# A separate ring of eight edge-list slots ahead of the four slots of gathered rows in a fused graph-attention kernel

## The chip, the cores and the metric

The program runs on one core of one Trainium2 chip. The core has five engines with a queue of instructions each: TensorE (PE, with its weight loads PEld), VectorE (DVE), ScalarE (ACT), GpSimd (POOL) and SyncE (SP), and 16 DMA engines that all of them share. The metric is the time of one execution on the device in microseconds, the median of several runs.

## What is computed

6250 nodes with 256 features and 200000 edges (src, dst), sorted by dst. The destinations are dense for low node numbers and thin out towards high ones. The layer norm of x feeds two branches: three graph-attention layers one behind the other, and a linear-attention block. Their sum is added to x, and a second layer norm feeds a feed-forward block of 8 experts with the two best weighted. The part that this case is about, the graph layer:

```python
def _gat_layer(x, W, al, ar, b, src, dst, apply_act):
    h = (x @ W).reshape(N_NODES, HEADS, HEAD_DIM)
    el = jnp.einsum('nhd,hd->nh', h, al)
    er = jnp.einsum('nhd,hd->nh', h, ar)
    e = jax.nn.leaky_relu(el[src] + er[dst], negative_slope=NEG_SLOPE_ATTN)
    m = jax.ops.segment_max(e, dst, num_segments=N_NODES)
    ex = jnp.exp(e - m[dst])
    s = jax.ops.segment_sum(ex, dst, num_segments=N_NODES)
    a = ex / s[dst]
    msg = h[src] * a[:, :, None]
    out = jax.ops.segment_sum(msg, dst, num_segments=N_NODES)
```

## The kernel before, in words

Nodes are cut into 49 tiles of 128 (loop variable `T`), edges into slots of 512 (`g`), each slot four chunks of 128 edges (`c`). For each of the three layers (`l`) a table in DRAM has, for each node, a row of 280 floats: the projected features with a one behind each head, and the logit terms. A *pair* (`n`) is one slot seen from one tile. As edges are sorted, a tile takes a few neighbouring slots: 57 pairs in tile 0, 24 in tile 1, 5 or 6 in the last ones, 440 pairs for 393 slots in a layer. The last slot of a tile is, at 47 of the 48 borders, also the first slot of the next (a *shared* slot); it is loaded and gathered once and used by two pairs. The control table `ctl` has a row per tile: the edge at which it starts, the first slot that it does not share (`unshared`), its last slot, `shift` (pair number minus slot number), its first slot, and two cuts of its slots into thirds, behind which other work is put.

The work of a slot goes through the engines like this:

- SP (L320 to L335) waits until the slot's ring place is free, loads `meta` (src and dst of 512 edges, 4 KB) and `dstb` (the 512 destinations as 16-bit numbers, copied to all 128 partitions, 128 KB), waits until both have landed and raises `meta_ready`. There are four places for everything (`RING`). The place is free when the messages of the pair four pair numbers back are done: `msg_ready` at L327 counts with the shift of the tile whose slot is loaded. At a shared border the first three new slots of a tile thereby wait for a pair later than the one that last used their place.
- POOL (L375 to L384) waits for `meta_ready` of the next slot, issues four indirect DMAs that gather 128 rows of the table each into `gat`, and behind the third of them announces the slot *before* (`gathered`, L360), once its rows have landed. So the announcement of slot g stands behind the wait for the edge list of slot g+1.
- DVE (`logits`, `messages`) waits for `uv_ready` of PE and for `gathered`, adds logits (`lg`, L955, L958), compares destinations for the next pair (`selT`, L943, from `dstb`), builds four selection matrices (`sel`, L963, from `meta`, each half behind `agg_done` of the pair before), waits for ACT's exponentials and multiplies the rows (`msg`, L972, two halves, each raising `msg_ready`).
- ACT (`weigh`) makes the exponentials (L471, L473).
- PE (`pairs`): `prepare(n + 1)` (L1225, 12 small matmuls out of `selT`), then `aggregate(n)` (L1249): two halves, each behind its `msg_ready`, of sel x msg, summed in `acc`. `after(part)` puts other work between thirds of a tile: the next layer's projection and the linear attention in layers 0 and 1, the experts (L1177, L1188) in layer 2.

Each engine takes its instructions in order; loops have run-time bounds.

## Time and profile before

| | |
|---|---|
| Median of three runs | 9743.75 us (9727.61 to 9778.39) |
| The profiled execution, its own time | 9719.24 us |
| Its span, first to last instruction | 9717.4 us |
| Mean granted TensorE clock | 0.803 |
| Busy: PE / DVE / POOL / ACT | 65% / 52% / 46% / 20% |
| Layer 0 / 1 / 2, about | 200 to 3160 / 3160 to 6130 / 6130 to 9650 us |

In the page, L12 is line 12 of the kernel. "Idle before" is how long an engine stood idle ahead of an instruction, and "<-" names what ended that: another engine's instruction and line, a DMA, "issue" where the profile shows no wait, and "remote" where a semaphore rose at that moment and the profile has no instruction that ended just then to put it down to. In the chain of waits the same appears as "another core or an unknown queue". The suffix q (SPq, POOLq, PEldq) marks the queue's own instructions. A row of the timeline merges repeats of one instruction.

### The profile page before, as it was taken

The numbers are of one execution on the slowest core, as the hardware profiler recorded it, in microseconds if no ns is written. First come the engines' busy times: TensorE is split into PE (matmuls) and PEld (weight loads), VectorE is DVE, ScalarE is ACT, GpSimd is POOL, SyncE is SP. The second block draws the span as 40 slices with busy tenths as digits, with TensorE's granted clock in tenths as the row PEclk, the third lists the DMA queues.
The fourth block names the chain that finished last, engine by engine and source line by source line (L and its number), as shares of the span: only waits on it lengthen the run. The fifth ranks groups of instructions, "written<-read, shape, count | busy, mean of one in ns | idle before, by whom it ended". The sixth has DMA issues, their size and how long they took to land.

```text
span 9717.4 us, 172782 instructions
## 1 busy us (share of the span) xinstructions
PE 6287.2 (65%) x38910; PEld 4899.6 (50%) x38911; DVE 5020.9 (52%) x14572; ACT 1955.3 (20%) x5913; POOL 4475.7 (46%) x4723
## 2 busy tenths in 40 slices
PE   3555555666666455555556566455777888889899
PEld 2434444444444333434444444334566667777778
DVE  4444555555555454555555566444554555555554
ACT  1000000101111000000000000001333444555555
POOL 0555554544444555555444444455444443333332
PEclk8677777777787676777777777777888899999999
DMA  4443433433333344333333333443333232222221
GB/s 157 109 106 99 103 101 101 106 96 98 99 100 93 102 106 99 101 101 98 98 97 97 98 98 96 94 104 99 92 89 83 78 78 76 74 72 70 66 67 44
DMA packets 638578, 909.85 MB, mean 94 GB/s; under 512 B 271425, under 2 KB 484554, under 8 KB 638410
## 3 DMA queue, kind: packets, MB, share of 16 engines
q0 software_dynamic: 226368, 676.39, 26.8%
q1 hardware_dynamic: 369546, 192.99, 8.4%
q10 hardware_dynamic: 42624, 40.02, 1.2%
q8 instruction: 16, 0.26, 0.0%
q14 instruction: 24, 0.20, 0.0%
HBM read 868.05 MB, written 40.87 MB: 94 GB/s over the span
## 4 chain that ended last, share of the span: by engine, by line
PE 28%; issue 18%; another core or an unknown queue 16%; DVE 15%; DVEq 12%; DMA 4%; ACT 4%; SPq 2%; ACTq 1%; POOL 1%; POOLq 0%
PE bank L1249 17%; DVE msg L972 6%; PE bank L1177 5%; PE bank L1188 4%; DVE sel L963 4%; DMA dstb<-dst_d 3%; DVEq L237 3%; DVEq L963 1%; DVE lg L955 1%; ACT region L429 1%; ACT L466 1%; DVEq L943 1%; DVEq L955 1%; SPq L328 1%
## 5 line engine op out<-in xcount | busy, mean ns | idle before, releaser
L353 POOL DMA_INDIRECT gat<-table,meta x4716 | 4474.7, 949 | 5152.8 <-SPq L335 3529.1
L1249 PE MATMUL bank<-msg,sel 128*128 128x264 f32 x10560 | 3667.1, 506 | 1751.7 <-DVE msg L972 1335.7
L1249 PEld LDWEIGHTS bank<-msg,sel 128*128 128x128 f32 x10560 | 2482.9, 247 | 2375.9 <-DVE msg L972 1432.7
L963 DVE TENSOR_SCALAR sel<-kc,base_i,meta 128x128 f32<-128x128 f32 x5280 | 1565.3, 355 | 1470.0 <-remote 799.9
L972 DVE TENSOR_TENSOR msg<-gat,bank 128x528 f32<-128x528 f32 x2640 | 1732.2, 697 | 576.5 <-ACT bank L473 480.2
L471 ACT ACTIVATE ex<-lg 128x32 f32<-128x32 f32 x1320 | 298.8, 226 | 6040.5 <-DVE lg L958 4609.5
L1225 PE MATMUL bank<-uvb,selT 128*128 (+1 forms) x15876 | 672.1, 172 | 1166.5 <-DVE selT L943 681.4
L1225 PEld LDWEIGHTS bank<-uvb,selT 128*128 128x128 bf16 x15876 | 617.0, 100 | 1566.9 <-issue 932.0
L955 DVE TENSOR_TENSOR lg<-gat,bank 128x64 f32<-128x64 f32 x1320 | 288.9, 219 | 1712.0 <-remote 901.4
L1177 PE MATMUL bank<-xT,w 128*128 128x128 f32 x6272 | 790.9, 281 | 18.0 <-issue 18.0
L1188 PE MATMUL bank<-w,region 128*128 128x256 f32 x3136 | 773.6, 390 | 42.2 <-ACT region L429 24.4
L1177 PEld LDWEIGHTS bank<-xT,w 128*128 128x128 f32 x6272 | 771.0, 197 | 49.0 <-issue 32.9
L1188 PEld LDWEIGHTS bank<-w,region 128*128 128x128 f32 x3136 | 577.1, 194 | 139.4 <-issue 41.1
L429 ACT ACTIVATE region<-bank,b 128x128 f32<-128x128 f32 x1568 | 443.8, 370 | 995.2 <-PE bank L1177 682.9
L943 DVE TENSOR_SCALAR selT<-dstb,kc 128x512 bf16 (+1 forms) x1323 | 498.3, 377 | 266.6 <-issue 158.3
L958 DVE TENSOR_TENSOR lg<-lg 128x32 f32<-128x32 f32 x1320 | 256.3, 194 | 112.3 <-issue 15.6
L1157 PE MATMUL bank<-zb 128*128 128x264 bf16 (+1 forms) x298 | 102.0, 344 | 323.3 <-DVE xn L986 243.2
L429 ACT ACT_TABLE_LOAD x237 | 304.1, 1283 | 6.0
L466 ACT ACT_TABLE_LOAD x236 | 302.8, 1283 | 4.3
L473 ACT ACTIVATE bank<-ex 128x32 f32<-128x32 f32 x1320 | 265.4, 201 | 89.9
L806 DVE SCALAR_TENSOR_TENSOR region<-bank,region 128x256 f32 (+1 forms) x343 | 165.2, 482 | 141.6 <-PE bank L1188 63.7
L1157 PEld LDWEIGHTS bank<-zb 128*128 128x128 bf16 x298 | 32.2, 108 | 345.5 <-DVE xn L986 252.4
(184 smaller groups left out, 2435.7 us busy)
## 6 DMA issues: line engine op xcount, KB each, us to landing
dstb<-dst_d SPq DMA_DIRECT2D x1179, 128.0 KB
gat<-table,meta POOLq DMA_INDIRECT x4716
meta<-in_edges SPq DMA_DIRECT2D x1179, 4.0 KB
table<-hrow ACTq DMA_DIRECT2D x98, 140.0 KB
w<-in_W SPq DMA_DIRECT2D x2, 4096.0 KB
table<-hrow SPq DMA_DIRECT2D x49, 140.0 KB, 1.8
region<-xnT_d ACTq DMA_DIRECT2D x50, 128.0 KB
region<-qT_d ACTq DMA_DIRECT2D x50, 128.0 KB
```

What stands on the lines that cost most here:

```text
L353: pool.indirect_dma_start(gat[:, r, c, :], None, table[l], bass.IndirectOffsetOnAxis(meta[:, r, c, 0:1].bitcast(U32), 0)).then_inc(s_done, 16)
L429: last = act.activation(gT[:, e % 2, k, :], bank[5 + e % 2][:, k * P:(k + 1) * P], ACT.Gelu, bias=b1[:, e * HB + k:e * HB + k + 1])
L466: act.activation(warm[:, 1:2], warm[:, 0:1], ACT.Exp)
L471: act.activation(ex[:], lg[:], ACT.Relu, scale=-1.0)
L943: dve_v.tensor_scalar(selT[:], dstb[:, bass.ds(g % RING, 1), :].rearrange("p a e -> p (a e)"), node[:, bass.ds(T, 1)], None, ALU.is_equal) ...
L955: dve_v.tensor_tensor(lg2[:], rows_of(g)[:, :, MSG:ROW], uv_p[:, 0:CH * UV].rearrange("p (c w) -> p c w", w=UV), ALU.add)
L963: dve_v.tensor_scalar(sel[:, c, :], iota, base_i[:, bass.ds(T, 1)], meta[:, bass.ds(g % RING, 1), c, 1:2].rearrange("p a w -> p (a w)"), A ...
L972: dve_v.tensor_tensor(msg[:, cs, :].rearrange("p c (h d) -> p c h d", h=H), rows_of(g)[:, cs, 0:MSG].rearrange("p c (h d) -> p c h d", h=H ...
L1177: last = pe.matmul(bank[5 + e % 2][:, k * P:(k + 1) * P], w1[:, e, c, k * P:(k + 1) * P], xT[:, 0, c, :], start=(c == 0), stop=(c == 1))
L1188: last = pe.matmul(y_psum[e % 2][:, 0:C], gT[:, e % 2, k, :], w2[:, e, k, :], start=(k == 0), stop=(k == HB - 1))
L1225: last = pe.matmul(uv_p[:, c * UV:(c + 1) * UV], selT[:, c * P:(c + 1) * P], uvb[:, part, bass.ds(T, 1), :].rearrange("p a b -> p (a b)"), ...
L1249: last = pe.matmul(acc[:, 0:MSG], sel[:, c, :], msg[:, c, :], start=False, stop=False)
```

## The change

The edge lists and broadcast destinations (`meta`, `dstb`) get a ring of `AHEAD` = 8 places, apart from the four of `gat`. SP's loop becomes: wait until the load before has landed; load `meta` and `dstb` of slot g; then wait until slot g-5 and all before it have been used up (`slot_free`, a new semaphore that starts at 8); then raise `meta_ready`. POOL gathers slot x when `meta_ready` is x+2 (before: x+1), which stands for three things: the edge list of x has landed, that of x+1 has been issued, and slot x-4 is used up. Who says that a slot is used up changes as well: before it was DVE's `msg_ready`; now PE raises `slot_free` by one in `aggregate`, behind its wait for the second half of the messages and ahead of the second half's matmuls. A tile's last pair raises nothing; the first pair of the next tile does it, once for a shared slot and twice otherwise, in a small loop with run-time bounds (`release_first`). POOL's loop is unrolled over eight slots instead of four, and the padding of slots goes to a multiple of 8 and one instead of 4 and one. That is the same 393 slots for these edges: 392 real ones and one of padding. `small` is cut from 512 to 256 columns to make room.

```diff
@@ SyncE, per layer @@
+                sp.sem_inc(meta_in[l], 16)
+                sp.sem_inc(dst_in[l], 16)
                 with sp.Fori(0, NT) as T:
                     with sp.Fori(unshared, last + 1) as g:
                         edge = edges_of(g, start, first)
-                        r = g % RING
-
-                        sp.wait_ge(msg_ready[l], 2 * (g + shift) + 2)
+                        r = g % AHEAD
+
+                        landed = sp.snap(16 * (g + 1))
+                        sp.wait_ge(meta_in[l], landed)
+                        sp.wait_ge(dst_in[l], landed)
                         sp.sem_inc(slot_taken, 1)
                         sp.dma_start(meta[...]).then_inc(meta_in[l], 16)
                         sp.dma_start(dstb[...]).then_inc(dst_in[l], 16)
-                        sp.wait_ge(meta_in[l], 16 * (g + 1))
-                        sp.wait_ge(dst_in[l], 16 * (g + 1))
+
+                        sp.wait_ge(slot_free[l], g + (AHEAD - RING))
                         sp.sem_inc(meta_ready[l], 1)
@@ GpSimd @@
-                pool.wait_ge(meta_ready[l], 1)
+                pool.wait_ge(meta_ready[l], 2)
                 for c in range(CH):
-                    gather_row(0, c, slot_in[l][0])
+                    gather_row(0, 0, c, slot_in[l][0])
                 with pool.Fori(0, rounds) as i:
-                    for j in range(RING):
-                        r = (j + 1) % RING
-                        pool.wait_ge(meta_ready[l], RING * i + j + 2)
+                    for j in range(AHEAD):
+                        m, r = (j + 1) % AHEAD, (j + 1) % RING
+                        pool.wait_ge(meta_ready[l], AHEAD * i + j + 3)
                         pool.sem_inc(round_taken, 1)
                         for c in range(CH):
-                            gather_row(r, c, slot_in[l][r])
+                            gather_row(m, r, c, slot_in[l][r])
                             if c + 2 == CH:
-                                announce(j, i + 1)
+                                announce(j % RING, 2 * i + j // RING + 1)
@@ VectorE @@
-                dve.sem_inc(msg_ready[l], AHEAD)
+                dve.sem_inc(slot_free[l], AHEAD)
                 def selectT(g, T):
-                    dve.wait_ge(meta_ready[l], g + 1)
+                    dve.wait_ge(meta_ready[l], g + 2)
@@ TensorE @@
-                def aggregate(n):
+                def aggregate(n, release):
                     for h in range(2):
-                        pe.wait_ge(msg_ready[l], 2 * n + (AHEAD + h + 1))
+                        pe.wait_ge(msg_ready[l], 2 * n + (h + 1))
+                        if h == 1:
+                            release()
                         for c in range(h * HALF, (h + 1) * HALF):
                             last = pe.matmul(acc[:, 0:MSG], sel[:, c, :], msg[:, c, :], start=False, stop=False)
+                    def release():
+                        pe.sem_inc(slot_free[l], 1)
+
+                    def release_first():
+                        if opening:
+                            release()
+                        else:
+                            pe.sem_inc(tile_opened, 1)
+                            with pe.Fori(unshared, first + 2):
+                                release()
+
                     prepare(n0 + 1, T)
-                    aggregate(n0)
+                    aggregate(n0, release_first)
                     for part, (begin, end) in enumerate(((n0 + 1, n1), (n1, n2), (n2, n3))):
                         with pe.Fori(begin, end) as n:
                             prepare(n + 1, T)
-                            aggregate(n)
+                            aggregate(n, release)
                     prepare(n3 + 1, T + 1)
-                    aggregate(n3)
+                    aggregate(n3, lambda: None)
```

## Rows read from the trace of the kernel before

**Rows 1.** The page's head: span, and busy time and share by engine.

```profile
span 9717.4 us, 172782 instructions
PE 6287.2 (65%) x38910; PEld 4899.6 (50%) x38911; DVE 5020.9 (52%) x14572; ACT 1955.3 (20%) x5913; POOL 4475.7 (46%) x4723
```

**Rows 2.** Stretches of the layers: length, busy PE, PEld, DVE, ACT, POOL, clock.

```profile
200.00:3160.00 2960.00, 1735.56 (x9994) 1268.59 (x9994) 1530.44 (x4472) 275.12 (x1174) 1491.69 (x1572) 0.75 0.40 101
3160.00:6130.00 2970.00, 1654.98 (x9796) 1233.75 (x9796) 1609.21 (x4428) 234.83 (x1077) 1490.88 (x1572) 0.73 0.39 98
6130.00:9650.00 3520.00, 2752.93 (x18391) 2294.21 (x18392) 1780.68 (x5379) 1374.12 (x3385) 1492.09 (x1572) 0.89 0.32 81
```

**Rows 3.** The page's chain that ended last, by engine.

```profile
PE 28%; issue 18%; another core or an unknown queue 16%; DVE 15%; DVEq 12%; DMA 4%; ACT 4%; SPq 2%; ACTq 1%; POOL 1%; POOLq 0%
```

**Rows 4.** Groups by line: busy, mean ns, idle before, by releaser.

```profile
L353 POOL DMA_INDIRECT gat<-table,meta x4716 | 4474.7, 949 | 5152.8 <-SPq L335 3529.1 <-issue 1591.5 <-DMA gat<-table,meta 15.6
...
L963 DVE TENSOR_SCALAR sel<-kc,base_i,meta 128x128 f32<-128x128 f32 x5280 | 1565.3, 355 | 1470.0 <-remote 799.9 <-PE bank L1249 481.3 <-issue 181.6
...
L955 DVE TENSOR_TENSOR lg<-gat,bank 128x64 f32<-128x64 f32 x1320 | 288.9, 219 | 1712.0 <-remote 901.4 <-issue 517.6 <-POOLq L360 166.2
```

**Rows 5.** Who waited on POOL's announcements (line 360), whole span: us, times.

```profile
  DVE lg L955: 211.1, 116
```

**Rows 6.** Timeline, layer 0, tile 2's end (last logits at 871.03).

```profile
861.95 1.30 DVE L972 TENSOR_TENSOR msg<-gat,bank 128x528 f32<-128x528 f32 x2
...
865.81 0.35 SPq L328 DMA_DIRECT2D meta<-in_edges  x1
...
867.69 2.05 PE L1249 MATMUL bank<-msg,sel 128*128 128x264 f32 x8 [1.12 <-DVE msg L972]
...
870.03 0.94 POOL L353 DMA_INDIRECT gat<-table,meta  x1 [5.39 <-SPq L335]
...
871.03 0.22 DVE L955 TENSOR_TENSOR lg<-gat,bank 128x64 f32<-128x64 f32 x1 [2.05 <-POOLq L360]
```

**Rows 7.** Timeline, start of layer 1.

```profile
3163.27 0.57 DVE L923 CAST uvb<-gat 128x784 bf16<-128x784 f32 x1
3164.38 0.34 SPq L328 DMA_DIRECT2D meta<-in_edges  x1
3164.93 0.34 SPq L330 DMA_DIRECT2D dstb<-dst_d  x1
3168.05 0.35 DVE L943 TENSOR_SCALAR selT<-dstb,kc 128x512 bf16<-128x512 uint16 x1 [4.21 <-SPq L335]
3168.29 0.94 POOL L353 DMA_INDIRECT gat<-table,meta  x1 [34.76 <-SPq L335]
```

**Rows 8.** PE's queue: loop branches, event instructions (ns min/median/max).

```profile
L1262 PEldq COMPARE_BRANCH  x1026: 67/207/222, 223.1 to 9640.5; - x171
...
L1183 PEldq EVENT_SEMAPHORE  x343: 51/51/51, 6701.7 to 9707.5; - x172
```

**Rows 9.** Timeline: a slow stretch in tile 0, layer 0.

```profile
526.97 0.60 DVE L963 TENSOR_SCALAR sel<-kc,base_i,meta 128x128 f32<-128x128 f32 x2 [3.90 <-remote]
...
531.88 0.60 DVE L963 TENSOR_SCALAR sel<-kc,base_i,meta 128x128 f32<-128x128 f32 x2 [4.32 <-remote]
```

**Rows 10.** Three stretches around it, columns as in group 2.

```profile
521.00:527.00 6.00, 0.46 (x12) 0.37 (x12) 0.82 (x4) 0.43 (x2) 4.57 (x5) 0.84 0.54 135
527.00:533.00 6.00, 0.00 (x0) 0.00 (x0) 1.68 (x5) 0.00 (x0) 2.99 (x4) 0.50 0.38 105
533.00:538.00 5.00, 4.20 (x20) 3.09 (x20) 2.79 (x10) 0.43 (x2) 0.00 (x0) 0.50 0.14 27
```

**Rows 11.** The page's DMA queues: gathers (q0), SP's transfers (q1).

```profile
q0 software_dynamic: 226368, 676.39, 26.8%
q1 hardware_dynamic: 369546, 192.99, 8.4%
```

**Rows 12.** SP's own waits, whole span: us in total, times, longest.

```profile
SPq L335 <- DMA dstb<-dst_d: 2433.0, 1109, 3.4
```

## What the change should do: the prediction, made blind

> **What bounds the kernel now.** I read the page's head first [rows 1]: no engine is full. PE is busy for 65% of the span, DVE for 52%, POOL for 46%. The stretches of the layers [rows 2] say where: in layers 0 and 1, PE and DVE are each busy for 52% to 59% of the time, POOL for half; in layer 2, with the experts, PE is at 2752.93 of 3520 us (78%). So the time of layers 0 and 1 is that of a chain which passes through several engines, and that of layer 2 is closer to PE's own. The chain of waits [rows 3] agrees: PE 28%, DVE 15% and its queue 12%, "another core or an unknown queue" 16%, and DMA 4%, SPq 2%, POOL 1%. What the change speeds up (SP, its loads, POOL) has a small part of it.
>
> POOL's row [rows 4] tempts to another reading: it idles for 5152.8 us, 3529.1 of them until SP raised `meta_ready` (L335). That idleness costs nothing unless someone waits for what POOL announces. So the next view is who waited on the announcements [rows 5]: DVE's logits (L955), 211.1 us, 116 times. The row of the logits themselves, seen from DVE's side [rows 4], gives them 166.2 us of idle time. That is 1.7% of the span and the pool from which the change can draw. Most of DVE's idleness is another: 901.4 us ahead of the logits and 799.9 us ahead of `sel` are "remote".
>
> Where the 166.2 us lie, the timeline at the end of tile 2 shows [rows 6]. The last pair's logits start at 871.03, after 2.05 us of waiting for L360. The announcement stands behind POOL's wait for the *next* slot's edge list, and those gathers started at 870.03, after 5.39 us in which POOL waited for SP. SP had issued the load at 865.81, for a ring place given free by the messages that ended at 861.95 + 1.30 = 863.25; by the late rule for shared borders that is one pair more than needed. I went through all pairs of the three layers: announcements that came over 0.5 us behind the messages before them are 76, nearly all at the last pair of a tile, and the others are in the first slots of a layer. Their waits sum to 118 us, and with the shorter ones to 137 us.
>
> **The slow stretches.** The "remote" waits matter as the ground against which everything here runs. Two halves of `sel` start at 526.97 and 531.88, each 3.90 or 4.32 us late [rows 9]. The wait between them is for four chunks' worth of half a pair on PE, for 4.9 us. In 521 to 533 POOL gathers without a pause (busy 4.57 of 6 us, then 2.99 of 6) and PE and DVE get almost nothing done; in 533 to 538 POOL rests and PE does 4.20 us of work in 5 [rows 10]. The DMA engines aren't full: their share is 0.54 and 0.38 in the slow stretches [rows 10]. Over all time slices, I find DVE in such a wait in about one slice in seven while POOL has gathered for less than 5 us on end, and in about half of them when it has for longer. This is a coincidence in time, not a shown cause.
>
> **The change part by part.** All sums are against the profiled execution, 9719.24 us (span 9717.4); it lies 24.5 us (0.25%) under the median of 9743.75, and the predicted time is the median plus the same difference.
>
> *The load leaves the path from a free place to its gathers, and the extra pair at shared borders goes.* Before: from SP's issue at 865.81 to the gathers 4.22 us [rows 6], and at the start of a layer 3168.29 - 3164.38 = 3.9 us [rows 7]. After: the list is there already, and the same event lets POOL start at once. Together with the pair saved (about 6.7 us: 2960 us for 440 pairs [rows 2]) the announcement at a tile's end comes some 10 us earlier, against a wait of 1.65 us in the mean (166.2 in 101 waits). These waits go as a whole. What is late next is PE: in [rows 6] its sums for the pair before began at 867.69 and need 2.05 us at the full clock, so it is done at 869.7, and `sel` of a pair whose logits start 2 us earlier meets that end without a wait; at half the clock the same work takes 3.9 us, which eats most of the gain. Mean clock is 0.73 to 0.89 [rows 2]. I take two thirds of 166.2 as recovered: -111 us (bounds: -50, and -211 if all of [rows 5] goes).
>
> *Start of a layer.* The first load goes out before DVE has finished the reference logits, and `meta_ready` = 2 asks only for the issue of the second. Before, `selT` started at 3168.05 and the gathers at 3168.29, after logits that ended at 3163.27 + 0.57 = 3163.84 [rows 7]. After, two issues (0.34 us each, 0.2 between them) and POOL's start of about 0.8 us (before, 3164.93 + 0.34 and 2.2 us of landing [rows 12] make 3167.5, and POOL starts at 3168.29): 2.5 us less, three times, -8 us. The gathers of the next slots are bound by one load after the other as before.
>
> *SP.* It has one load in flight at a time, as before; landing costs it 2433.0 us of waiting in 1109 waits, 2.2 us each [rows 12], now while nobody needs it. Its cycle of about 5 us for a slot is under the 7.5 us for which a slot lasts (2960 us for 393). Costed at nothing; the cover is that difference.
>
> *PE's release.* An instruction of 51 ns [rows 8] on PE's queue for each of 1320 pairs. It waits for the second half of the messages, and only the second half's matmuls are queued behind it; before, the first of those held the same wait. Cover: the four chunks of the first half, 1.0 us, against messages that come 0.65 us after the first half's (1.31 for both). At each tile's first pair the small loop comes on top, with a branch of 207 ns at the median [rows 8] and some register instructions of 40 ns, in all 0.34 us, 147 times: 50 us uncovered at the full clock, nothing at half of it. I take +15 us. In a slow stretch every instruction of PE's is dear: half a pair's four chunks, eight instructions and their loads, took the 4.9 us of [rows 9], 0.6 us each. My 1320 + 8 x 147 = 2500 instructions are 3.2% of PE's 77821 [rows 1]; 3.2% of the 901.4 + 799.9 = 1701 us [rows 4] is 55 us. Bounds 0 and 55, taken +30 us, since DVE's waits aren't all for PE. The release also follows PE's order now: if PE is late, the place comes free late, by up to the 4.9 us of [rows 9]. Who waits for that is SP, then POOL, then an announcement that has come 10 us earlier, of which its waits need 2 to 4; costed at nothing.
>
> *POOL and DVE.* POOL's loop over eight slots saves half of its loop ends, and DVE's instructions stay the same. Nothing, both.
>
> Sum: -111 - 8 + 15 + 30 = **-74 us**: 9645 us for the profiled execution, **9670 us** for the median.
>
> *A rule against it.* After the change, each slot's load travels beside gathers, where before POOL stood waiting for it. The loads hold 8.4% of the DMA engines' time and the gathers 26.8% [rows 11]; 8.4% of 9717 us over 1179 slots is 0.7 us of all engines for a slot, which the 6 us or more that the announcement now has to spare swallow. The Trainium skill, "DMA: Bandwidth & Descriptors", section "Queues, rings and completion order", says that a DMA engine takes turns, packet by packet, between the queues that have work, so a load in the same moment does slow a gather. By that rule, too, the sum stays as it is; only where the turns reach the engines' own work, as rival 2 has it, would it change.
>
> **The rivals.** *Rival 1: the wait changes its name.* The 111 us are taken by what comes next at the tile's end (PE at half clock, a slow stretch that the gathers now fall into), and the additions to PE remain. For it: "remote" and "issue" waits at L955 are 1419.0 us, eight times those for POOL [rows 4]; DVE is nearly always held by something else. Price: -50 + 45 - 8 = -13 us, 9731 us. Against: at the tile's end in [rows 6], PE is no later than DVE.
>
> *Rival 2: the gathers run on end, and slow stretches grow.* Before, SP's cycle of load and landing puts a pause between bunched gathers (5.39 us in [rows 6]); the change takes these pauses away, and POOL follows each release at once. If gathers without a pause are the cause of the slow stretches [rows 9, 10], their 1701 us grow. It decides from a growth of 4% (74 us); with 12%, +204 us, the sum is +130 us: 9874 us; with 9%, 9823. Laying the new rule over the old times of release, I find POOL's time in runs over 10 us on end up by a fifth in layers 0 and 2 and down a little in layer 1, worth between 0 and +100 us by the shares above. Against: the gathers' sum, the places for rows and the pairs' pace stay, and POOL's total of 4474.7 us [rows 4] is the same; runs on end happen when PE and DVE are fast, and end when the four places are full.
>
> *Rival 3: it does more than it says.* Gathers spread evenly and ahead take a part of the slow stretches with them: 8% of 1701 is -136 us, with the sum -210 us: 9534 us.
>
> *That it doesn't do what it says* could be only if POOL's idle time until SP stayed. The order of waits excludes that in a steady run: the load of the next slot is issued two slots' use ahead, 15 us, of which it needs 5.
>
> **How the numbers follow.** Forecast (9600 to 9695, a gain of 50 to 145 us): 0.43. Rival 1 (9695 to 9790): 0.31. Rival 2 (over 9790): 0.20. Rival 3 (under 9600): 0.06. The range that leaves out two in ten: from 9575, which takes in half of rival 3, up to 9825, where two thirds of rival 2 lie below (its 0 to +100 us and PE's upper bounds). A measurement of this kernel can tell 0.5% (49 us) from no change. Faster by more: 0.43 + 0.06 = 0.49. Within: 0.31. Slower by more: 0.20.
>
> **What would show it right or wrong.** In the profile after: waits of DVE's logits for POOL under 40 us instead of 166; POOL's idle time no longer put down to SP after a landing, but to SP after a release from PE; SP's waits for landings gone or small, waits for `slot_free` in their place; logits at a tile's last pair with no wait over 1 us; selT and the first gathers of a layer 2 to 3 us behind L923. Right for rival 1: the same, with the span as before and "remote", "issue" and PE's rows larger by 100 us. Right for rival 2: "remote" ahead of L955 and L963 clearly over 1701 us in sum, and gathers in longer rows. Wrong altogether: waits for POOL as large as before, or PE idle ahead of L1249's second halves by some tenths of a microsecond each, the price of the release where I hid it.

## The result, and the profile after

The changed kernel takes **10094.1 us** at the median of 4 runs (10083.29 to 10096.91), the kernel before 9745.04 us on the same chip: ratio **1.0352**, 95% interval 1.0323 to 1.0381. It is slower by 3.5%; 9670 us was forecast and 9825 us was the upper end of the range. Run twice more, the change gave 1.0363 (1.0321 to 1.0405) and, on a chip where the kernel before takes only 7759.59 us, 0.9961 (0.9947 to 0.9976). This second kind of chip has a section of its own below; where nothing is said, a run comes from a chip on which the kernel before takes 9727 to 9875 us.

The head of the page of the changed kernel, and its chain of what ended last, answering [rows 1] and [rows 3]:

```profile
span 10081.5 us, 174415 instructions
PE 6430.9 (64%) x38910; PEld 5010.5 (50%) x38911; DVE 5049.9 (50%) x14572; ACT 1960.1 (19%) x5913; POOL 4495.8 (45%) x4723
...
PE 31%; another core or an unknown queue 22%; issue 15%; DVE 14%; DVEq 11%; ACT 5%; ACTq 1%; DMA 0%; SPq 0%; POOL 0%; POOLq 0%; PEldq 0%
```

DMA and SPq have left the chain (4% and 2% before), as they were meant to. "Another core or an unknown queue" has grown from 16% to 22%. The stretches of the layers, with the columns of [rows 2]:

```profile
200.00:3240.00 3040.00, 1738.64 (x9994) 1275.49 (x9994) 1534.62 (x4471) 276.08 (x1174) 1499.49 (x1572) 0.76 0.39 98
3240.00:6256.00 3016.00, 1710.62 (x9796) 1267.40 (x9796) 1610.11 (x4429) 234.90 (x1077) 1499.33 (x1572) 0.73 0.39 97
6256.00:10014.00 3758.00, 2837.92 (x18390) 2364.78 (x18391) 1804.69 (x5380) 1377.76 (x3384) 1495.91 (x1572) 0.87 0.31 76
```

Every layer is longer: by 80, 46 and 238 us. The granted clock differs by 0.02 at most (0.89 before and 0.87 now in layer 2, where PE is busy for 85 us more), so it explains a small part at best. The groups by line, answering [rows 4]: gathers, PE's sums, `sel`, logits:

```profile
L371 POOL DMA_INDIRECT gat<-table,meta x4716 | 4494.7, 953 | 5492.7 <-SPq L347 4081.8 <-issue 1367.9 <-remote 31.0
L1269 PE MATMUL bank<-msg,sel 128*128 128x264 f32 x10560 | 3793.7, 518 | 2420.9 <-DVE msg L990 1849.6 <-issue 565.1
L981 DVE TENSOR_SCALAR sel<-kc,base_i,meta 128x128 f32<-128x128 f32 x5280 | 1566.1, 352 | 2223.0 <-remote 1395.6 <-PE bank L1269 635.2 <-issue 176.3
L973 DVE TENSOR_TENSOR lg<-gat,bank 128x64 f32<-128x64 f32 x1320 | 287.2, 218 | 1519.5 <-remote 915.3 <-issue 493.9 <-PE bank L1243 78.1
```

The busy times of POOL's and DVE's rows stand still (within 20 us each). PE's sums are busy for 126.6 us more, in records whose ends are modelled; their row before was this:

```profile
L1249 PE MATMUL bank<-msg,sel 128*128 128x264 f32 x10560 | 3667.1, 506 | 1751.7 <-DVE msg L972 1335.7 <-issue 415.9
```

What moved most are the idle times. "Remote" ahead of `sel` rose from 799.9 to 1395.6 us, ahead of the logits from 901.4 to 915.3: 1701.3 to 2310.9, **+610 us, or 36%**. Against it, the logits have 192.5 us less of idle time in all (1712.0 to 1519.5). Their waits for POOL are gone, in the table of waits:

```profile
DVE lg L973 <- POOLq L378: 24.5, 33, 7.3
```

It was 166.2 us in 101 waits [rows 4]. So the part that the change aims at works: 142 us of these waits are gone, where the sum had 111. SP's own waits (us in total, times, longest) show the rest of the design, against 2433.0 us of waits for landings [rows 12]:

```profile
SPq L347 <- PEq L1278: 1938.5, 475, 10.1
SPq L347 <- PEq L1285: 1536.8, 144, 20.1
SPq L339 <- DMA dstb<-dst_d: 301.8, 246, 2.6
```

And the start of layer 1, answering [rows 7]:

```profile
3243.63 0.57 DVE L941 CAST uvb<-gat 128x784 bf16<-128x784 f32 x1
3245.19 0.34 SPq L340 DMA_DIRECT2D meta<-in_edges  x1
3245.74 0.36 SPq L342 DMA_DIRECT2D dstb<-dst_d  x1
3246.26 0.35 DVE L961 TENSOR_SCALAR selT<-dstb,kc 128x512 bf16<-128x512 uint16 x1 [2.06 <-SPq L347]
3246.49 0.95 POOL L371 DMA_INDIRECT gat<-table,meta  x1 [39.13 <-SPq L347]
```

From the end of L941 to the first gather it is 2.29 us (3246.49 - 3244.20); before it was 3168.29 - 3163.84 = 4.45. That is 2.2 us saved, and at the starts of layers 0 and 2 it is 2.0 us each; 2.5 us were forecast.

A stretch of layer 0 shows what the added waits are. Timeline of the changed kernel, with the wait ahead of each row in brackets:

```profile
2029.84 2.05 PE L1269 MATMUL bank<-msg,sel 128*128 128x264 f32 x8 [1.13 <-issue]
...
2031.34 0.95 POOL L371 DMA_INDIRECT gat<-table,meta  x1 [0.53 <-issue]
...
2032.02 0.60 DVE L981 TENSOR_SCALAR sel<-kc,base_i,meta 128x128 f32<-128x128 f32 x2
2032.20 0.66 PE L1243 MATMUL bank<-uvb,selT 128*128 x12 [0.31 <-DVE selT L961]
2032.59 0.95 POOL L371 DMA_INDIRECT gat<-table,meta  x1 [0.30 <-issue]
2033.84 0.95 POOL L371 DMA_INDIRECT gat<-table,meta  x1 [0.30 <-issue]
2034.54 0.70 SPq L340 DMA_DIRECT2D meta<-in_edges  x1
2035.10 0.95 POOL L371 DMA_INDIRECT gat<-table,meta  x1 [0.30 <-issue]
2037.38 0.01 SPq L342 DMA_DIRECT2D dstb<-dst_d  x1
2037.56 0.60 DVE L981 TENSOR_SCALAR sel<-kc,base_i,meta 128x128 f32<-128x128 f32 x2 [4.94 <-remote]
```

The second half of `sel` needs the second half of the sums that PE began at 2029.84. By PE's record they end at 2031.89, and PE begins the next pair's matmuls at 2032.20; DVE sees the semaphore at about 2037.5. The same wait stands in [rows 9]. SP is slow here too: its two issues are 2.84 us apart, at the layer's start 0.55. POOL is not: its gathers start every 1.25 us as always. The Trainium skill, "Perfetto Trace Analysis", section "Tensor Engine Instruction (MATMUL, LD_WEIGHTS)", says that the end of a matmul is computed by the profiler, and that the semaphore is raised only when PSUM has acknowledged the bytes. This row agrees in so far as end and semaphore are over 5 us apart; whether the work or its announcement is late, it can't tell. The record of the semaphores in the same trace puts the delay on PE's side: the last matmul of the sums raises its semaphore at 2037.41, and the last of the twelve matmuls begun at 2032.20 (by its record over at 2032.86) raises another at 2037.59, while DVE's own, raised by `selT` (over at 2032.06), comes at 2032.08. DVE isn't slow here; it waits. Around it, stretches with the columns of [rows 2]:

```profile
2026.00:2032.00 6.00, 4.76 (x26) 3.35 (x24) 3.80 (x12) 0.34 (x3) 4.45 (x5) 0.73 0.47 113
2032.00:2038.00 6.00, 0.66 (x12) 0.51 (x12) 1.06 (x5) 0.09 (x1) 3.13 (x4) 0.83 0.54 137
2038.00:2043.00 5.00, 4.17 (x10) 3.15 (x11) 2.12 (x6) 0.42 (x2) 0.00 (x0) 0.52 0.04 10
```

It is the picture of [rows 10]: a slow stretch of 5 us while POOL gathers, and work as soon as it rests. But POOL gathers in the first of the three too, at full pace for PE and DVE. Counted over the trace, the waits of over 3.5 us ahead of a half of `sel` went from 84 to 193, in 2640 halves (223 in c1, a second run of the same kernel).

### The profile page after: what moved, and what is told of

Read it like the earlier page. It is cut to its first block, busy times and chain, and to the rows that moved or that the text cites. A ratio compares the mean times of both kernels' runs of the same rounds, so it can differ in the third digit from the quotient of the medians.

```text
span 10081.5 us, 174415 instructions
## 1 busy us (share of the span) xinstructions
PE 6430.9 (64%) x38910; PEld 5010.5 (50%) x38911; DVE 5049.9 (50%) x14572; ACT 1960.1 (19%) x5913; POOL 4495.8 (45%) x4723
## 4 chain that ended last, share of the span: by engine, by line
PE 31%; another core or an unknown queue 22%; issue 15%; DVE 14%; DVEq 11%; ACT 5%; ACTq 1%; DMA 0%; SPq 0%; POOL 0%; POOLq 0%; PEldq 0%
PE bank L1269 21%; DVE msg L990 6%; PE bank L1195 5%; DVE sel L981 4%; PE bank L1206 3%; DVEq L239 3%; DVEq L981 1%; ACT L484 1%; ACT region L447 1%; DVE lg L973 1%; ACT L447 1%; DVEq L1009 1%; PE bank L1243 1%; DVE region L1049 1%
## 5 line engine op out<-in xcount | busy, mean ns | idle before, releaser
L1269 PE MATMUL bank<-msg,sel 128*128 128x264 f32 x10560 | 3793.7, 518 | 2420.9 <-DVE msg L990 1849.6
L1269 PEld LDWEIGHTS bank<-msg,sel 128*128 128x128 f32 x10560 | 2542.2, 253 | 3098.1 <-DVE msg L990 1950.0
L981 DVE TENSOR_SCALAR sel<-kc,base_i,meta 128x128 f32<-128x128 f32 x5280 | 1566.1, 352 | 2223.0 <-remote 1395.6
L1243 PE MATMUL bank<-uvb,selT 128*128 (+1 forms) x15876 | 646.5, 172 | 793.3 <-DVE selT L961 486.8
L973 DVE TENSOR_TENSOR lg<-gat,bank 128x64 f32<-128x64 f32 x1320 | 287.2, 218 | 1519.5 <-remote 915.3
L1195 PE MATMUL bank<-xT,w 128*128 128x128 f32 x6272 | 846.1, 290 | 99.0 <-issue 98.6
L1195 PEld LDWEIGHTS bank<-xT,w 128*128 128x128 f32 x6272 | 813.1, 204 | 147.5 <-issue 131.6
L1149 PE MATMUL bank<-wext,xT 128*128 128x280 f32 x588 | 178.7, 429 | 3.0 <-ACT xT L496 0.9
```

The lines of the kernel that those rows point to most:

```text
L973: dve_v.tensor_tensor(lg2[:], rows_of(g)[:, :, MSG:ROW], uv_p[:, 0:CH * UV].rearrange("p (c w) -> p c w", w=UV), ALU.add)
L981: dve_v.tensor_scalar(sel[:, c, :], iota, base_i[:, bass.ds(T, 1)], meta[:, bass.ds(g % AHEAD, 1), c, 1:2].rearrange("p a w -> p (a w)"), ...
L1195: last = pe.matmul(bank[5 + e % 2][:, k * P:(k + 1) * P], w1[:, e, c, k * P:(k + 1) * P], xT[:, 0, c, :], start=(c == 0), stop=(c == 1))
L1243: last = pe.matmul(uv_p[:, c * UV:(c + 1) * UV], selT[:, c * P:(c + 1) * P], uvb[:, part, bass.ds(T, 1), :].rearrange("p a b -> p (a b)"), ...
L1269: last = pe.matmul(acc[:, 0:MSG], sel[:, c, :], msg[:, c, :], start=False, stop=False)
```

## The experiments

The theory after the result (T) is that the loss is made by the gathers, and by *where in a pair's work* they start: the new rule starts them early, and they then fall on PE's sums and on the first half of the next pair. Its rivals: the instructions added to PE's queue (P); the release that now follows PE's order (O); and slow stretches that have nothing to do with gathers (N).

### Is it the gathers at all?

**g1_one_gather.** The kernel before, with one gather of four. It leaves out three quarters of the gathered rows, so its output isn't the layer's; a constant stands in their place.

```diff
-                        for c in range(CH):
-                            gather_row(r, c, slot_in[l][r])
-                            if c + 2 == CH:
-                                announce(j, i + 1)
+                        gather_row(r, 0, slot_in[l][r])
+                        announce(j, i + 1)
```

> The kernel before with one gather of 128 rows for each slot instead of four; chunks 1 to 3 of the rows keep a constant that is written once a layer, so three quarters of the gathered data are left out. Everything else runs as before. If the gathers make the slow stretches (waits put down to 'remote' ahead of logits and sel, 1701 us in the kernel before): under 400 us of them, and the time 7800 to 8700 us. If they come from elsewhere (SyncE's loads, PE itself): over 1200 us of them, and 9400 to 9700 us.

A single execution took 7654.02 us, beside 9727.17; that is less than the lowest of the range that was expected. Its sums, `sel` and logits by line:

```profile
L1248 PE MATMUL bank<-msg,sel 128*128 128x264 f32 x10560 | 3271.2, 462 | 1054.4 <-DVE msg L971 1049.4 <-issue 5.0
L962 DVE TENSOR_SCALAR sel<-kc,base_i,meta 128x128 f32<-128x128 f32 x5280 | 1519.9, 343 | 333.7 <-PE bank L1248 329.6
L954 DVE TENSOR_TENSOR lg<-gat,bank 128x64 f32<-128x64 f32 x1320 | 289.1, 219 | 1214.8 <-POOLq L360 784.2 <-issue 257.1 <-PE bank L1224 165.7
```

"Remote" is gone from both of DVE's lines. All else of the pair's work, and SP's 193 MB of loads, is there. N falls: on this chip, three quarters of the gathers cost the kernel about 2070 us, while the logits' waits for POOL were 166.2 us before [rows 4] (and are 784.2 us in g1, where the announcement stands behind the only gather). Whether it is POOL's issuing or the 507 MB that the gathers move, this run doesn't tell.

### PE's release taken apart

In the cuts below, the number added behind the slot differs from run to run because each semaphore starts from its own value. Lines left out are marked with three dots.

**a1_dve_release.** The change, but the place is given free by the messages, as in the kernel before; nothing added on PE.

```diff
-                        sp.wait_ge(slot_free[l], g + (AHEAD - RING))
+                        sp.wait_ge(msg_ready[l], 2 * (g + shift) + 2)
```

> The changed kernel, with the release taken off PE: SyncE waits for msg_ready (raised by VectorE's messages) of the same pair, as the kernel before did, and PE's instructions are those of the kernel before. The eight-slot ring, the early loads and the early gathers stay. Theory 1 (early gathers: they now start with PE's sums of the same pair and lengthen the slow stretches there): as slow as the changed kernel or slower, since gathers start up to 1 us earlier still: 10050 to 10200 us. Theory 2 (the release instruction on PE, which holds up PE's queue, is the loss): the loss goes and the gain of the earlier announcements is left: 9620 to 9720 us.

**a2_before_pe_release.** The kernel before, plus the change's instructions on PE (each pair's `sem_inc`, the loop at a tile's first pair), which nobody waits for.

```diff
+                        if h == 1:
+                            release()
```

> The kernel before with PE's release instructions alone: PE raises slot_free behind the wait for the second half of the messages, and in the small loop at a tile's first pair, but nobody waits for it. Ring, loads and gathers are those of the kernel before. Theory 1: 9745 to 9800 us (at most the 15 + 30 us of the prediction). Theory 2: 10000 to 10150 us.

**a3_late_release.** The change, with PE's release behind the second half's matmuls in program order.

```diff
-                        if h == 1:
-                            release()
                         for c in range(h * HALF, (h + 1) * HALF):
...
                         last.then_inc(agg_done[l], 1)
+                    release()
```

> The changed kernel with PE's release moved behind the matmuls of the second half, so that it holds no matmul of the pair up. The gathers start some 1 us later in program order. Theory 1: as slow as the changed kernel, 10000 to 10150 us. Theory 2: most of the loss goes, 9650 to 9800 us.

**a7_dve_release_pe_extra.** a1 with a2's instructions on PE.

> The kernel with the release by VectorE's messages (9900 us) with PE's release instructions put back, raising a semaphore for which nobody waits. If the 190 us between that kernel and the changed one are the price of PE's instructions: 10050 to 10130 us. If they come from where the gathers start (the release by PE comes later, or later still in a slow stretch) and the instructions cost the 0.4% that they cost in the kernel before: 9900 to 9960 us.

| kernel | us | ratio to before (95%) | remote ahead of `sel` / logits, us |
|---|---|---|---|
| a1, messages release | 9899.77 | 1.0156 (1.0112 to 1.0200) | 1375.3 / 642.1 |
| a2, before with PE's extras | 9790.87 | 1.0040 (1.0014 to 1.0066) | 784.9 / 966.3 |
| a3, release in program order behind the sums | 10089.85 | 1.0342 (1.0294 to 1.0389) | 1409.6 / 868.5 |
| a7, a1 with PE's extras | 9937.15 | 1.0234 (1.0186 to 1.0282) | 1323.9 / 703.1 |

P has a size: 0.4% in a2, and 0.8% by a7 against a1 (the two intervals overlap, and the runs are from two chips). It isn't the cause. With nothing on PE, a1 is still slower than before by 1.6%, and its remote waits sum to 2017 us. That is between its two expectations: neither all of the loss stays nor all of it goes. a3 equals the change in time, and its gathers lie where the change's do (the table in the next section): in these runs a bare `sem_inc` behind the matmuls in program order releases no later than one ahead of them, so it doesn't tell that the sums are done. What separates a7 (1.0234) from the change (1.0352) is only which event frees the place: one pair earlier at shared borders, and PE's queue for DVE's messages. That is 1.2%, and O may hold it; the run meant to split it (a13) comes below.

### Gathers tied to the sums

**a4_sums_release.** The change, but SP waits for the semaphore on the last matmul of the pair's sums (`agg_done`). Nothing added on PE.

```diff
-                        sp.wait_ge(slot_free[l], g + (AHEAD - RING))
+                        sp.wait_ge(agg_done[l], 2 * (g + shift) + 4)
```

> The changed kernel, but SyncE lets POOL gather only when PE's sums of the pair that used the slot have ended (it waits for agg_done, raised by the last matmul), with no release instruction on PE. Gathers so start 1 to 4 us after the messages, behind the sums of their pair, and 1 to 4 us earlier than in the kernel before. Theory 1, if it is the meeting of gathers with the sums of the same pair that costs: most of the loss goes, 9650 to 9850 us; if it is run-on gathers wherever they lie: 9950 to 10150 us. Theory 2: 9620 to 9720 us. This run is of use beside the first one, which has no release on PE either.

**a6_half_sums.** As a1, and then the first half's sums as well.

```diff
-                        sp.wait_ge(slot_free[l], g + (AHEAD - RING))
+                        used = sp.snap(2 * (g + shift) + 2)
+                        sp.wait_ge(msg_ready[l], used)
...
+                        sp.wait_ge(agg_done[l], used + 1)
```

> As the kernel whose gathers wait for the end of the sums (9270 us), but SyncE waits for msg_ready of the pair and for the first half of its sums alone, so that the gathers meet the second half of the sums. No release instruction on PE. Theory 1a (the loss is in the overlap of gathers with the sums of the same pair, in proportion): between the two neighbours, 9270 and 9900 us, at about 9500 to 9700 us. Theory 1b (what counts is only that the gathers are tied to PE's progress at all, so that a slow stretch stops the gathers that make it): near 9270 us, under 9400 us.

**b1_before_sums_release.** The kernel *before* (four places, load behind the release), with a4's wait.

```diff
-                        sp.wait_ge(msg_ready[l], 2 * (g + shift) + 2)
+                        sp.wait_ge(agg_done[l], 2 * (g + shift) + 6)
```

> The kernel before, ring of four and load behind the release, with the one difference that SyncE waits for the end of PE's sums of the pair (agg_done) and not for its messages. The gathers start 1 to 4 us later than before. If the gain of 4.9% is that of a release tied to the sums, whatever the ring: 9300 to 9550 us. If it needs the early load of the eight-slot ring (gathers right behind the sums, before the next pair's): 9700 to 9950 us, since the announcements at the tile ends come later still.

| | freed by messages | freed by the end of the sums |
|---|---|---|
| load behind the release (4 places) | 1 (kernel before, 9745) | b1: 10004.85 us, 1.0321 (1.0262 to 1.0380) |
| list loaded ahead (8 places) | a1: 9899.77 us, 1.0156 (1.0112 to 1.0200) | **a4: 9270.07 us, 0.9505** (0.9464 to 0.9547) |

a6 lies beside a4: 9314.49 us, 0.9594 (0.9549 to 0.9640), in the range expected if the tie to PE's progress is what counts. Each of the two edits alone makes the kernel slower, and both together make it 5% faster than before. Neither a4 (under all of its ranges) nor b1 (over both) was forecast. Rows of a4, then of b1, by line:

```profile
L981 DVE TENSOR_SCALAR sel<-kc,base_i,meta 128x128 f32<-128x128 f32 x5280 | 1551.2, 356 | 1044.4 <-PE bank L1267 467.0 <-remote 349.6 <-issue 218.2
L973 DVE TENSOR_TENSOR lg<-gat,bank 128x64 f32<-128x64 f32 x1320 | 287.7, 218 | 1833.8 <-remote 1196.8 <-issue 362.4 <-POOLq L379 165.0
```

```profile
L963 DVE TENSOR_SCALAR sel<-kc,base_i,meta 128x128 f32<-128x128 f32 x5280 | 1563.0, 355 | 1400.8 <-remote 672.0 <-PE bank L1249 543.9 <-issue 181.1
L955 DVE TENSOR_TENSOR lg<-gat,bank 128x64 f32<-128x64 f32 x1320 | 289.6, 219 | 2143.8 <-remote 1027.9 <-issue 504.1 <-POOLq L360 493.6
```

In a4, the remote waits ahead of `sel` are a quarter of the change's; of the long ones (over 3.5 us) 7 are left of 193. But those ahead of the logits are the largest of all, 1196.8 us. The two together are 1546.4 us, only 155 us under the kernel before (1701.3), while the span is 444 us shorter (9272.9); the rest of the gain lies in no single row. In b1 the load stands between the sums and the gathers, and the logits wait for POOL for 493.6 us, 327 us more than before; its remote waits sum to 1699.9 us, as before. So b1's loss goes with the waits for POOL, and not, as the change's, with remote waits. Worked out from the starts of all gathers, the share of time in which POOL gathers, by the time from the start of a pair's messages:

| from messages' start, us | -1..0 | 0..1 | 1..2 | 2..3 | 3..4 | 4..5 | 5..6 | 6..7 |
|---|---|---|---|---|---|---|---|---|
| before | .57 | .57 | .68 | .66 | .64 | .59 | .51 | .65 |
| change | .50 | .49 | .46 | .69 | .83 | .80 | .84 | .86 |
| c1, the change again | .50 | .49 | .46 | .69 | .83 | .80 | .85 | .87 |
| a3 | .50 | .50 | .47 | .67 | .83 | .81 | .84 | .87 |
| a1 | .48 | .43 | .35 | .78 | .86 | .85 | .87 | .89 |
| a4 | .53 | .76 | .73 | .71 | .68 | .63 | .63 | .73 |
| a6 | .72 | .71 | .68 | .65 | .63 | .66 | .73 | .78 |
| b1 | .58 | .64 | .64 | .60 | .60 | .68 | .74 | .71 |

Change, a3 and a1 pack the gathers from 2 us behind the messages' start on; before, a4 and a6 spread them. How long the gathers run on end is a poorer guide. Counting gathers whose starts lie under 2 us apart as one run, the share of their time in runs of over 10 us is 53% before, 65% in a1, 75% in the change, 43% in a4, 50% in a6 and 62% in b1; but c1, the change again at the same time and with the same remote waits (2280.9 us), has 62%.

T fits these runs in this form: released with the messages and with the list at hand, the gathers come in a pack that falls on the sums and the next `sel`. Shown is that the event which releases them makes a difference of 6% (a1 against a4); that the overlap is the way in which it does is argued from the table. Whether the place in time counts, or that a4's gathers can't run ahead of PE, these runs don't separate.

### Spacing the gathers out

Three kernels put a pause between gathers, to see whether the pack is what hurts: **a5_paced** (the change), **a9_sums_paced** (a4), and **a8_fixed_delay** (a1, the pause only ahead of a slot's four, six times).

```diff
                             gather_row(m, r, c, slot_in[l][r])
+                            pool.drain()
+                            pool.memset(pace[:], 0.0)
```

> The changed kernel with a drain and a small memset (some 0.3 us) on POOL behind each gather, so that four gathers take some 6.5 us and not 5.0. If it is the rate of gathers back to back that makes the slow stretches: under 9850 us (changed kernel: 10094). If only the overlap with the sums counts and not the rate: 10050 to 10200 us.

> The kernel whose gathers wait for the end of the sums (9270 us), with the pause of 0.3 us behind each gather. A candidate for a faster version: if the rate counts beside the tie, 9000 to 9200 us; if it doesn't, 9270 to 9400 us, as the announcements then come later.

> The kernel with the release by VectorE's messages (9900 us), with six drains and memsets on POOL ahead of each slot's gathers: a fixed delay of 2 to 4 us between release and gathers. If the gain of the release by sums is one of phase alone (gathers 2 to 4 us later): 9250 to 9500 us. If it needs the tie to PE's progress (in a slow stretch no new gathers start until PE is through): 9750 to 10050 us.

18942.48 us (1.9203, 1.9124 to 1.9282), 18504.27 us (1.8762, 1.8685 to 1.8839) and 11967.45 us (1.2131, 1.2081 to 1.2180): they failed as experiments, since the pause was far longer than the memset in it. POOL's rows in a8:

```profile
1000.02 0.94 POOL L373 DMA_INDIRECT gat<-table,meta  x1 [0.30 <-issue]
1003.12 2.37 POOL L402 MEMSET pace<- 128x240 f32 x6 [2.16 <-issue]
```

Between the gather and the memset, where the drain stands, POOL is idle for 2.16 us. With a drain behind each gather POOL became the bound, as a5's rows show:

```profile
L984 DVE TENSOR_SCALAR sel<-kc,base_i,meta 128x128 f32<-128x128 f32 x5280 | 1478.4, 362 | 11.7 <-PE bank L1272 1.6 <-issue 0.7
L976 DVE TENSOR_TENSOR lg<-gat,bank 128x64 f32<-128x64 f32 x1320 | 292.2, 221 | 13311.3 <-POOLq L379 12899.9 <-issue 411.4
```

What they do show: in a5 and a9, with gathers 4 us apart, there is not one remote wait at `sel` or the logits, and in a8, with four gathers on end and then a pause of about 5 us, 67.4 us are left. With everything waiting for POOL this is weak evidence for T.

### A chip without slow stretches

Six runs fell on two chips on which the kernel before takes 7762 and 7760 us. Four of them were meant to separate time from order, and to take the rest of the release apart. What was expected of them was worked out for the first kind of chip, so none of it is confirmed or refuted:

**a10_split_gathers**: a6 with two gathers behind the first half's sums and two behind the second's.

```diff
                         sp.sem_inc(meta_ready[l], 1)
+                        sp.wait_ge(agg_done[l], used + 2)
+                        sp.sem_inc(meta_ready[l], 1)
```

> A candidate, built on the kernel that waits for half of the sums (9314 us): SyncE raises meta_ready twice for a slot, once when the first half of the sums of the pair has ended (POOL issues two gathers), once when the second half has (the other two). Bursts of gathers halve to 2.5 us, and each is tied to PE's progress. If run-on bursts make the slow stretches and the tie ends them: 9050 to 9250 us, with less 'remote' than 1574 us (the 420.7 + 1153.0 of the half-sums kernel). If the size of the bursts doesn't matter: 9270 to 9400 us.

**a11_two_us_delay**: a1 with a 1 KB load and a wait for it behind the release.

```diff
                         sp.wait_ge(msg_ready[l], 2 * (g + shift) + 2)
...
+                        sp.dma_start(pace[:], ...).then_inc(paced[l], 16)
+                        sp.wait_ge(paced[l], 16 * (g + 1))
```

> The kernel with the release by VectorE's messages (9900 us), and a small load of 1 KB with the wait for its landing between that release and meta_ready: a fixed delay of about 2 us, without the drains that made the earlier delay kernel (11967 us) bound by POOL. If the gain of the sums' release (9270 us) is one of phase: 9250 to 9500 us. If it is the tie to PE's progress, which a fixed delay doesn't have: 9750 to 10000 us, between the kernel without delay and the kernel before with its 4 to 5 us.

**a12_next_half**: a4 waiting for half a pair more.

```diff
-                        sp.wait_ge(agg_done[l], 2 * (g + shift) + 4)
+                        sp.wait_ge(agg_done[l], 2 * (g + shift) + 5)
```

> The kernel that waits for the end of the sums (9270 us), waiting for the first half of the next pair's sums as well: gathers start some 3 to 6 us later, still tied to PE. If the tie is all: 9270 to 9450 us, with some waits for POOL's announcements. If the phase behind the sums is what counts: 9500 to 9900 us.

**a13_pe_release_late_rule**: the change, and SP waits for the messages by the old late rule too.

```diff
                         sp.wait_ge(slot_free[l], g + (AHEAD - RING))
...
+                        sp.wait_ge(msg_ready[l], 2 * (g + shift) + 2)
```

> The changed kernel (10094 us, slot_free raised by PE, exact at shared borders), with SyncE waiting for msg_ready by the old late rule as well, so that the first three new slots of a tile are again a pair late. The kernel with the late rule and PE's unused releases took 9937. If the exact rule (gathers at a tile's start closer together) makes the difference of 150 us: 9930 to 9980 us. If it is the release in PE's order: 10060 to 10130 us.

Then three more of kernels already known, to have the change on both kinds of chip: **c1_change_again**, **c2_change_third** (both the change unaltered) and **c3_split_again** (a10 unaltered).

> The changed kernel once more, beside the kernel before, on whatever chip comes. The last batch ran on a chip on which the kernel before takes 7762 us and shows no 'remote' waits. If the loss of 3.5% is made by slow stretches alone: on a chip that shows them (before near 9740 us) a ratio of 1.03 to 1.04 again; on one without (before near 7760 us) a ratio of 0.985 to 1.00, as the changed kernel with the late rule had 0.9973. If the chip makes no difference to the ratio: 1.03 to 1.04 on both.

> The changed kernel a third time, for the case that the chip is one without slow stretches (before near 7760 us): then 0.985 to 1.00 if the loss belongs to the slow stretches, 1.03 to 1.04 if it doesn't. On a chip with them (before near 9740 us): 1.03 to 1.04 as twice before, and then the question for the other kind of chip stays open.

> The kernel with split gathers, each half tied to PE's sums, beside it. It took 0.9941 of the kernel before on the chip without slow stretches. On a chip with them (before near 9740 us): 9050 to 9250 us if short bursts tied to PE's progress are worth more than whole ones (9270 us), 9270 to 9400 us if the size of a burst doesn't matter.

| kernel | us | before, same chip | ratio (95%) |
|---|---|---|---|
| c1, the change | 10101.29 | 9744.73 | 1.0363 (1.0321 to 1.0405) |
| c2, the change | 7726.08 | 7759.59 | **0.9961** (0.9947 to 0.9976) |
| a13, change with the late rule | 7741.89 | 7761.88 | 0.9973 (0.9961 to 0.9985) |
| a10 / c3, split gathers | 7713.60 / 7709.74 | 7761.88 / 7759.59 | 0.9941 (0.9922 to 0.9960) / 0.9932 (0.9908 to 0.9956) |
| a11, delay of a small load | 7898.29 | 7761.88 | 1.0184 (1.0161 to 1.0208) |
| a12, half a pair later | 8250.65 | 7761.88 | 1.0627 (1.0606 to 1.0649) |

c1 and c2 came out as expected if the loss belongs to the slow stretches.

From the head of c2's page, and its lines:

```profile
PE 5899.2 (76%) x38910; PEld 4654.4 (60%) x38911; DVE 5018.9 (65%) x14572; ACT 1958.3 (25%) x5913; POOL 4487.0 (58%) x4723
...
L981 DVE TENSOR_SCALAR sel<-kc,base_i,meta 128x128 f32<-128x128 f32 x5280 | 1551.1, 360 | 361.9 <-PE bank L1269 346.1 <-issue 0.4
L973 DVE TENSOR_TENSOR lg<-gat,bank 128x64 f32<-128x64 f32 x1320 | 288.1, 218 | 1171.5 <-POOLq L378 556.7 <-issue 448.7 <-PE bank L1243 158.5
```

Same instructions, same data, and no remote wait. It is the same picture as in g1, reached without leaving out a gather: on this kind of chip no such wait goes with the gathers, though 88% of their time is in runs of over 10 us. Here the change is 0.4% faster; as there is no trace of the kernel before from such a chip, which of its waits that saves is not shown. Layers 0 and 1 last some 2200 us each for 393 slots, 5.6 us a slot, and POOL needs 4 x 1.25 = 5.0 us of them, so POOL is nearly the bound and the logits wait for it; delays of the gathers then cost at once, as a11 and a12 show (the logits wait 951.3 and 1475.7 us for POOL). None of these runs says what a10 to a13 do where there are slow stretches. That stays open, and with it the 1.2% between a7 and the change, and the question of time against order. What makes the two kinds of chip differ, nothing in the traces tells.

One more difference goes with the slow stretches. The increments of semaphores that the instructions carry can be counted against the rises that the trace has. In the change these are 15266 of 20428 (75%), in the kernel before 15000 of 19105 (79%), in a4 14185 of 19108 (74%). In c2 they are 20248 of 20428 (99%), in g1, a5 and a9 over 99%, in a8 89%. So where DVE has remote waits, a fifth to a quarter of the rises is missing from the trace. That makes "remote" a less certain label there, as it is worked out from those rises; the lengths of the waits don't rest on it. It also leaves a rival that no run tests: every execution timed in these experiments was recorded too, so the recording itself may have a part in the slow stretches.

## Why the prediction was wrong, point by point

**Direction and size.** -74 us were forecast, +364 us came (span 10081.5 against 9717.4). Rival 2, with a chance of 0.20, was the case. Its deciding point was a growth of the slow stretches' waits by 4%; they grew by 36%, three times the 12% of its dearer case. The range was also labelled wrongly: by the prediction's own chances, 9575 to 9825 us leaves out one in ten (a third of rival 2 and half of rival 3), and not two.

**The step that failed** is the one that costs the gathers' earliness at nothing. The change part by part counts what waits for an announcement, and stops there: "the gathers' sum, the places for rows and the pairs' pace stay" was taken to mean that their effect on PE and DVE stays. What the runs showed in its place: the remote waits grew by 610 us, and which event releases the gathers is worth 6% with the same ring and loads (a1 at 1.0156, a4 at 0.9505). The trace of before held the warning: "remote" was 1701 us [rows 4], ten times the pool of 166.2 us, and about half of the slices with long gather runs were slow ones, against one in seven. A quantity ten times as large as the gain, tied by coincidence to the very engine that is being moved, can't be put in at zero with a range of 0 to +100. That range came from new release rules laid over old times, and it priced the length of POOL's runs. That was the wrong quantity: the share of the gathers' time in long runs was 75% in one trace of the change and 62% in the other, with the same loss, while the place of the gathers behind the messages came out the same in both. The overlay also kept the old pace of the pairs, so it couldn't see a slower pair releasing later; how much that adds, no run shows. By which route the gathers hold PE up stays open.

**The waits for POOL.** Right in kind: 166.2 to 24.5 us, under the 40 that were named; -142 us against -111. That PE is late next was right too: the waits of `sel` for the end of the sums rose from 481.3 to 635.2 us.

**Start of a layer.** -2.0 to -2.2 us against -2.5 for each of three; right.

**SP.** Right: waits for landings fell from 2433.0 to 301.8 us, with waits for a release in their place.

**PE's release.** +45 us were set (15 for the loop, 30 in slow stretches); a2 measures 0.4% (39 us), a7 against a1 0.8% (76 us) with overlapping intervals. By a2 the term was about right, by a7 too small. That the place comes free late, which was costed at nothing, is not settled: between a7 and the change there are 1.2%.

**The rule against it, of taking turns between queues.** It was to leave the sum as it is unless it reached the engines' own work. The DMA engines' share was 0.54 in the slow stretch at 2032 to 2038 us, and 0.47 in the fast one before it, so the load on the DMA engines doesn't separate the two; on the other kind of chip the page of c2 has the gathers' queue at 34.5% of the engines against 26.8% [rows 11], and no such wait. No run here ties the slow stretches to that rule.

**Rival 1** (9731 us): of its signs (remote and PE's rows larger by 100 us, the span as before) one is half seen: the wait did change its name, but came back six times as large. **Rival 3** (9534 us) had its lever with the wrong edit: a4 takes 468 us out, 155 us of it visibly from remote waits, but with gathers that wait for the sums and not with gathers further ahead. **That it doesn't do what it says** didn't happen.

**A condition that wasn't named at all:** the chip. The sum without slow stretches (-142 for the waits, -6 for the layers' starts, +39 for PE by a2) has the sign of c2, which gains 33 us; there the logits go on waiting for POOL (556.7 us), so the gain can't be the whole sum. The agreement in sign is no proof of the terms.

## What to carry to other kernels

When the trace shows waits that no instruction of the program explains, and they are larger than the gain in view, settle first which engine's activity they go with, by taking most of that activity away once; an edit that lets that engine start earlier can move them, whatever it does to the wait it aims at. Loading ahead and the event that releases the transfer are two decisions: on the first kind of chip each alone cost 1.6% to 3.2%, and together they gave 5% (a4 was not run on the second kind). So try a prefetch with its release tied to the busy engine's finished work before dropping it, and measure on more than one chip if the times of an unchanged kernel differ between them.

## What the runs showed of the hardware that was not expected

- One program (the kernel before) takes 9727 to 9875 us on four chips and 7760 to 7762 us on two others. The change's spans are 10081.5 and 7722.3 us, 2359 us apart, with 2310.9 us of remote waits on the first kind and none on the second. The gathers bring these waits on: with a quarter of the gathers the first kind of chip is at 7654 us.
- In the slow stretch at 2032 us, PE and SP are late at once: over 5 us from the recorded end of PE's sums to the rise of their semaphore, and 2.84 us between two issues of SP that otherwise are 0.55 us apart, at a DMA share of 0.54. DVE's own semaphore comes in time, and POOL gathers at full pace.
- In traces with such stretches 21 to 26% of the semaphore rises are missing (11% in a8, with its 67 us of remote waits), in those without them under 2%.
- A bare semaphore increment behind matmuls on PE's queue releases no later than one ahead of them (1.0342 against 1.0352, with the gathers in the same place); waiting for the increment that the last matmul carries gives 0.9505.
- With a drain behind an indirect gather POOL is idle for 2.16 us in a8 before its next instruction, and for 0.30 us between two gathers without one.
